# Reordering the PE and ACT queues of a fused two-layer transformer block: z transpose, output projection, context product, weight rounds and second scores

## The reference

```python
x = x + wkv(w, u, layernorm(x), ctx)              # a recurrence over the rows
x = x + fake_quant_ffn(layernorm(x))              # 256x256, 8-bit fake quantisation
x = x + cross_and_self_attention(layernorm(x), ctx)
x = x + gated_linear_attention(layernorm(x))
```

```python
ln = _ln(x)                                        # "z"; then 4 scaled copies rounded to fp8
q, k, v, qx = four projections of the fp8 copies   # 16 heads of 128; 8 groups of k and v
kx, vx = split(cond @ w_kv_x)                      # from the context
q, k, qx, kx = each normalised over its head's 128 features
core = softmax(q k^T / sqrt(128)) v
xout = softmax(qx kx^T / sqrt(128)) vx
x += fp8(concat(core, xout) / smooth) @ wproj^T * scales
```

## Time and profile before

| | us |
|---|---|
| median of 3 executions | 684.87 |
| lowest, highest | 682.72, 685.02 |
| profiled execution: its own time | 684.33 |
| profiled execution: span from first to last instruction | 682.5 |

### The profile page before, as it was taken

How to read it: one execution, slowest core, us unless ns; L and a number is a source line. 1 busy time by engine, 2 the same in 40 slices (tenths; PEclk the granted TensorE clock), 3 DMA queues, 4 the chain that set the end, 5 groups by cost and what they waited for, 6 DMA issues and landing times.

```text
span 682.5 us, 13253 instructions
## 1 busy us (share of the span) xinstructions
PE 614.7 (90%) x4523; PEld 492.6 (72%) x4567; DVE 528.4 (77%) x1305; ACT 401.6 (59%) x1339; POOL 250.1 (37%) x338
## 2 busy tenths in 40 slices
PE   4456999999999999989999999989999999999936
PEld 3245777777877878877788778768887788877725
DVE  7998688988786768858877788868664676868697
ACT  4255766767777646647667366567563666554531
POOL 2115664334333453323345433333332444430233
PEclk9997999999999999989999999999999999999977
DMA  8236452343672203331233222332342323110001
GB/s 269 79 148 215 149 167 71 104 163 119 210 259 101 101 15 105 109 104 74 105 122 103 90 101 101 101 102 101 102 162 100 102 101 101 16 33 1 1 0 62
DMA packets 36972, 72.86 MB, mean 107 GB/s; under 512 B 3342, under 2 KB 28586, under 8 KB 32810
## 3 DMA queue, kind: packets, MB, share of 16 engines
q1 hardware_dynamic: 36720, 72.00, 31.7%
q10 hardware_dynamic: 186, 0.02, 0.0%
HBM read 59.41 MB, written 12.60 MB: 106 GB/s over the span
## 4 chain that ended last, share of the span: by engine, by line
PE 73%; DVE 13%; issue 6%; ACT 5%; POOL 2%; DMA 0%; another core or an unknown queue 0%; DVEq 0%; POOLq 0%; ACTq 0%
PE bank L691 14%; PE bank L591 14%; PE bank L711 13%; PE bank L598 8%; PE bank L663 4%; PE bank L677 3%; PE bank L735 3%; PE bank L692 2%; PE bank L725 2%; PE bank L821 2%; PE bank L481 1%; PE bank L830 1%; DVE Cb L1749 1%; PE bank L750 1%; ACT KTt L1093 1%
## 5 line engine op out<-in xcount | busy, mean ns | idle before, releaser
L711 PEld LDWEIGHTS bank<-V,Pt 128*128 128x128 f32 x1024 | 127.7, 191 | 27.1 <-DVE Cb L1749 15.7
L1069 ACT ACTIVATE square<-bank 128x128 bf16<-128x128 f32 x372 | 98.4, 276 | 75.8 <-PE bank L591 46.7
L711 PE MATMUL bank<-V,Pt 128*128 128x129 f32 x1024 | 136.6, 276 | 2.2 <-DVE Cb L1749 1.2
L691 PE MATMUL bank<-QT,KTt 128*128 128x512 f32 x256 | 132.5, 599 | 2.9 <-POOL diag L1332 1.5
L1332 POOL TENSOR_TENSOR diag<-identb,nm 128x512 bf16<-128x512 bf16 x64 | 66.9, 1045 | 169.5 <-DVE nm L1734 169.4
L1052 ACT ACTIVATE Pt<-bank 128x512 f32<-128x512 f32 x128 | 76.8, 600 | 72.2 <-remote 46.3
L1734 DVE TENSOR_REDUCE nm<-bank 128x2 f32<-128x512 f32 x128 | 82.0, 682 | 36.2 <-PE bank L677 36.1
L1317 POOL TENSOR_TENSOR rs<-ve,mhalf 128x6 f32<-128x6 f32 x64 | 86.8, 1356 | 5.3
L591 PE MATMUL bank<-WQ,xq 128*128 128x256 f32 x512 | 80.4, 300 | 1.9 <-DVE xq L1645 1.3
L1749 DVE SCALAR_TENSOR_TENSOR Cb<-bank,ro,ism 128x128 bf16<-128x128 f32 x256 | 78.1, 347 | 4.5
L591 PEld LDWEIGHTS bank<-WQ,xq 128*128 128x128 f32 x512 | 68.1, 192 | 13.6 <-issue 7.6
(11 more groups left out here) (233 smaller groups left out, 1017.9 us busy)
## 6 DMA issues: line engine op xcount, KB each, us to landing
WQ<-wq_split SPq DMA_DIRECT2D x24, 1024.0 KB, 7.7
WH<-wh_split SPq DMA_DIRECT2D x24, 384.0 KB, 8.9
wq_split<-WQ SPq DMA_DIRECT2D x8, 1024.0 KB, 4.6
ism<-smooth_inverse SPq DMA_DIRECT2D x32, 256.0 KB, 6.4
wst<-in_L_xattn_wproj SPq DMA_DIRECT2D x16, 256.0 KB, 4.0
wh_split<-WH SPq DMA_DIRECT2D x8, 384.0 KB, 3.4
wst<-in_L_xattn_wq SPq DMA_DIRECT2D x8, 256.0 KB, 5.0
wst<-in_L_xattn_wqx SPq DMA_DIRECT2D x8, 256.0 KB, 5.1
```

The source lines that it names most:

```text
L691: nc.tensor.matmul(o[:], KTt[u % 2][:, x, t * P:(t + 1) * P], QT[u % 2][:, x, :], start=True, stop=False)
L711: last = nc.tensor.matmul(o[:, h * (P + 2):h * (P + 2) + P + 1], Pt[:, x, k, h * S + t * P:h * S + (t + 1) * P], V[u % 2][:, x, k, 0:P + 1 ...
L1069: last = A(square[:, t, h], head(t, h), ACT.Square, accum_out=ss[:, t, h:h + 1])
```

## The change

The instructions are the same; their order on PE and on ACT is another. DVE, POOL and SP keep theirs.

- `SCORES_FIRST` goes from 6 to 1: from unit 1 on, `scores(u, 0, 1)` follows `scores(u, 0, 0)` directly, ahead of `project(u + 1, 1)`, and so do the exponentials on ACT.
- The context product of tile 0 of unit `u + 2` (`project_values`) leaves the end of `project(u + 2, 0)` and stands ahead of `guard(u + 1, 0)`.
- In the units with `g == 1` from batch 1 on, `weigh(u, 0, 0)` goes ahead of `project_out(b - 1, 1)`, and `turn_outputs(u - 1)` behind `turn(u + 1)`; ACT's copy of it stands between the third and the fourth part of `evacuate`.
- `turn_z` stands behind `project(u + 2, 0)` in batches 1 and 2, and so does its read on ACT.
- In unit 7 the three weight rounds each come one place earlier, the first right behind `project(8, 0)`. In unit 6 ACT reads the second round ahead of `over_scales`.

```diff
@@ -233,7 +233,7 @@
 
         NARROW_BEHIND = {0: 3, 1: 4, 4: 6, 5: 7}
 
-        SCORES_FIRST = 6
+        SCORES_FIRST = 1
 
         def round_of(u, i):
 
@@ -608,7 +608,16 @@
                 else:
                     pe.wait_ge(s[f"ring{u % RING}_loaded"], loads_before(u))
 
-            def project(u, t):
+            def project_values(u):
+
+                b, g = divmod(u, G)
+                if u < G:
+                    pe.wait_ge(s["wc_evac"], u + 1)
+                if g == 0:
+                    pe.wait_ge(s["v_evac"], b + 1)
+                project_context(u, 0)
+
+            def project(u, t, context=True):
 
                 b, g = divmod(u, G)
                 if t == 0:
@@ -628,8 +637,10 @@
                 for p in range(2, 4):
                     if g == 0 and t == 0:
                         pe.wait_ge(s["xq4_ready"], 4 * b + p + 1)
-                    project_head(u, t, p)
-                project_context(u, t).then_inc(s["qkv_done"], 1)
+                    last = project_head(u, t, p)
+                if context:
+                    last = project_context(u, t)
+                last.then_inc(s["qkv_done"], 1)
 
             def project_first_context():
 
@@ -884,6 +895,8 @@
                     scores(u, 0, 1)
                 if u + 1 == G:
                     project(u + 1, 0)
+                    for r in round_of(u, 0):
+                        weights(*r)
                 project(u + 1, 1)
                 if 1 in steps:
                     turn_context(nb)
@@ -894,33 +907,38 @@
                 if u < SCORES_FIRST:
                     scores(u, 0, 1)
                 scores(u, 1, 0)
+                weigh(u, 0, 0)
                 if g == 1 and b:
                     project_out(b - 1, 1)
-                weigh(u, 0, 0)
-                if u >= 1 and not (g == 1 and b):
+                elif u >= 1:
                     turn_outputs(u - 1)
                 scores(u, 1, 1)
                 if 5 in steps:
                     ffn(nb)
                 weigh(u, 0, 1)
+                for r in round_of(u, 1 if u + 1 == G else 0):
+                    weights(*r)
+                turn(u + 1)
                 if g == 1 and b:
                     turn_outputs(u - 1)
-                for r in round_of(u, 0):
+                weigh(u, 1, 0)
+                for r in round_of(u, 2 if u + 1 == G else 1):
                     weights(*r)
-                turn(u + 1)
-                weigh(u, 1, 0)
-                for r in round_of(u, 1):
-                    weights(*r)
+                if u + 2 != G and u + 2 < UNITS:
+                    project_values(u + 2)
                 guard(u + 1, 0)
                 weigh(u, 1, 1)
-                if 6 in steps:
+                if 6 in steps and not b:
                     turn_z(nb)
                 if u + 2 != G and u + 2 < UNITS:
-                    project(u + 2, 0)
+                    project(u + 2, 0, False)
                 if 0 in steps:
                     turn_h(nb)
-                for r in round_of(u, 2):
-                    weights(*r)
+                if 6 in steps and b:
+                    turn_z(nb)
+                if u + 1 != G:
+                    for r in round_of(u, 2):
+                        weights(*r)
                 guard(u + 1, 1)
                 if g == 0 and u:
                     project_out(b - 1, 0)
@@ -1184,28 +1204,34 @@
                 if u >= 1 and not (u % G == 1 and u > G):
                     outputs(u - 1)
                 exps(u, 1, 1)
-                for r in round_of(u, 0):
+                for r in round_of(u, 1 if u + 1 == G else 0):
                     weights(*r)
+                if 1 in steps:
+                    differences(nb, 0, 1)
+                evacuate(u + 1, range(3))
                 if u % G == 1 and u > G:
                     outputs(u - 1)
-                if 1 in steps:
-                    differences(nb, 0, 1)
-                evacuate(u + 1)
-                if 7 in steps:
+                evacuate(u + 1, (3,))
+                if 7 in steps and u >= G:
                     over_scales(nb, (2, 3))
-                for r in round_of(u, 1):
+                for r in round_of(u, 2 if u + 1 == G else 1):
                     weights(*r)
+                if 7 in steps and u < G:
+                    over_scales(nb, (2, 3))
                 if 1 in steps:
                     differences(nb, 2, 3)
-                if 6 in steps:
+                if 6 in steps and u < G:
                     turned_z(nb)
                 if u + 2 != G and u + 2 < UNITS:
                     squares(u + 2, 0)
                     values(u + 2, 0)
                 if 0 in steps:
                     turned_h(nb)
-                for r in round_of(u, 2):
-                    weights(*r)
+                if 6 in steps and u >= G:
+                    turned_z(nb)
+                if u + 1 != G:
+                    for r in round_of(u, 2):
+                        weights(*r)
 
             u = UNITS - 1
             exps(u, 0, 0)
```

## The result

The changed kernel takes **672.3 us** by the median of 4 executions (672.11 to 672.55). The kernel before, measured beside it, takes 684.62 (682.72 to 685.02). The ratio is 0.9826, 95% interval 0.9807 to 0.9845: 12.3 us faster. The prediction was 669.5, range 665.5 to 676.5. So sign and range hold, and 2.8 us of the forecast gain are missing. The profiled execution took 672.11, its span is 670.3 us.

A forecast was written before the change was run, and what follows sets the result against it. PE was taken to bound the kernel, except in batch 0 and some units of batches 1 and 2, where DVE's chain is as long. Terms summed to 15.0 us off 684.33, 669.3; forecast 669.5, range 665.5 to 676.5.

The forecast's parts named there:

- z transposes: Units 12 and 20: projection and context product fill PE's wait ahead of the transposes of z, 2 x 2.64 = 5.3 us.
- Clock: Unit 12: with the long wait gone, the stretch at the lower clock behind it goes too, 2.8 us, from 0 to 2.8.
- Context product at the guards: Ends of units 0, 8, 9, 16, 17, 25: it fills PE's waits at the guard, 0.9 plus five times 0.4, 2.9 us.
- What that move delays: First guard up to 0.92 us later; DVE's gapless chains in units 10, 14, 18, 22 lose: -0.4 us, between -3 and +1.
- Batch 0: Units 1 to 5: losses from later guards and gains from earlier second scores cancel, 0 us, between -2.5 and +1.5.
- Unit 9 and its like: Units 9, 17, 25: output transposes no longer wait for their bank, 3 x 0.72 = 2.2 us, between 1.6 and 2.4.
- Weight rounds: Units 6 and 7: PE's waits for ACT ahead of weight rounds go, 2.2 us net, between 0.8 and 3.0.
- DVE takes the place of the waits: Rival: DVE's gapless chains in batches 0 to 2 leave 8.5 us of the gain, 676; chance 0.20 for 671.5 to 677.
- Slower: Rival: the first guard's 0.92 us passes whole through DVE and POOL in 29 places, about 695 us; chance 0.04.
- The clock is not won: Rival: the clock drop is chance or comes again at unit 1's longer diagonal wait, 672.3 us; chance 0.12.

The follow-up runs named there:

- z_only: The kernel before with only the z transposes, and ACT's read of them, moved behind the projection in batches 1 and 2: 675.78 us against 683.27, ratio 0.9885.
- after_pool_late: The changed kernel with POOL's first difference of the recurrence also waiting for DVE's pair of maxima with shifted rows: 670.51 us, ratio 0.98.

## Why the prediction was right in sign and 2.8 us off

Point by point, forecast against the lengths of bodies:

- **z transposes, 5.3.** Bodies 12 and 20 give 2.55 each without the clock, 5.1. Right; and DVE's scaling was not put off by the moved guard.
- **Clock, 2.8.** Right in the profile (2.80), and close for the median: z_only wins 7.5 by the medians of the chip, 5.5 of it without the clock, which leaves 2.0 (2.4 by the ratio). That the profile of before held a whole drop is luck: four profiles with both waits lost 2.80 + 0, 1.58 + 0, 0 + 1.65 and 1.50 + 1.61 us in bodies 12 and 20, so the picture of one drop in one place was wrong. In the rule of the Trainium skill that was weighed (TensorE: Matmul & The Clock Gate, What's actually happening) the half rate is the default and activity releases it; that each of two equal waits must then cost a drop was the prediction's own reading of it. That a drop can come at both is shown (1.50 and 1.61); that one must is refuted by the zeros, each behind a full wait.
- **Context product at the guards, 2.9.** The guards' records are 0.62 in the five later places, as forecast, and still 0.86 in body 0, where 0.9 was to be won and 0.69 was. The others gave 0.49 in bodies 8 and 16 (seen only once the loss there is gone), and 0.30 in bodies 9, 17 and 25: 2.6 in all. Nearly right.
- **What that move delays, 0.4 lost.** This is the step that failed. Bodies 14 and 22 are longer by 0.3 as worked out, 10 and 18 by 0.38 instead of 0.2, and body 29, which was not looked at, by 0.27. Bodies 13 and 21 win some 0.2 instead of 0.3, and nine others 0.06 each. What is missing altogether is 0.95 us in each of bodies 8 and 16, 1.9 us: 0.84 of each is DVE held up by POOL. The prediction followed DVE's queue with fixed durations, and one of them went from 0.48 to 1.32. The trace of before had such a case: the first step of the fp8 rounding (L1761), 0.42 us by the median, took 1.36 at the ends of bodies 8 and 16, beside a POOL instruction.

```profile
232.70 1.09 POOL L1297 TENSOR_TENSOR tmp<-tmp,vT 128x512 f32<-128x512 f32 x1
232.70 1.36 DVE L1761 TENSOR_SCALAR Cb<-Cb 128x1024 bf16<-128x1024 bf16 x1
```

  With it the term comes to -2.6 instead of -0.4, two thirds of the 3.3 us that the bodies fall short of the forecast (15.0 less 11.7).
- **Batch 0, 0.** The second scores gave 0.6 to 0.95, and the later guards took 1.4 (body 0 aside), so -0.8 by the first figure. The loss of 0.7 foreseen at the second weighing of unit 3 is there: it starts 9.46 us after the body's start instead of 8.70. What wasn't seen is the next step in the same body. PE and DVE of the changed kernel:

```profile
129.24 0.94 PE L722 MATMUL bank<-V,Pt 128*128 128x129 f32 x6 [0.20 <-DVE Cb L1775]
...
137.42 0.49 PE L562 MATMUL bank<-cen,wst 128*128 128x128 f32 x2 [0.38 <-DVE rest L1733]
...
134.32 1.29 DVE L1760 TENSOR_REDUCE nm<-bank 128x2 f32<-128x512 f32 x2 [0.63 <-PE bank L688]
...
136.25 1.11 DVE L1733 SCALAR_TENSOR_TENSOR rest<-bank,vec,WH 128x128 f32<-128x128 f32 x4
```

  DVE waits 0.63 for the later guard (L688) before its maxima; behind them in its queue are an output scaling and the read of a weight round (L1733), and the next round on PE (L562) needs that bank: 0.38. 0.76 and 0.38 make up body 3's 1.12. I listed what is queued on DVE behind the maxima, but not the weight round. Of body 5's 0.38 the trace shows the place: its output transposes (L736) wait 0.49 for the last step of DVE's rounding (L1791). In body 6, 0.34 longer, the second weighing waits 0.16 for an output scaling; the rest is open.
- **Unit 9 and its like, 2.2.** 1.03 in each of three bodies less 0.29 in two: 2.5, just above the upper bound of 2.4. The gap from the weighing to the next step was 1.68 less 0.89 = 0.79, the upper end; 0.24 more came from the steps around. The give-back in body 10 was not named.
- **Weight rounds, 2.2.** 1.13 and 1.09: 2.2. Right.
- **The rivals.** "DVE takes the place of the waits" describes the missing part, at a third of its size. "Slower" needed 0.55 us a place in 29 places; six places lose over 0.35 and nine gain 0.06. Its mechanism is real in body 3. "The clock is not won" has 672.3, the very time measured, and still isn't the reason: its price was a drop that comes again, and no stretch of the units ran below 1.00 in the changed kernel's profile.
- **The sum itself.** 684.33 less 15.0, plus the 0.5 that the prediction names, is 669.8, not 669.5.

By bodies these are 5.1 + 2.8 + 2.6 - 2.6 - 0.8 + 2.5 + 2.2 = 11.8, against 11.7 in the table; the other 0.5 of the 12.2 us between the two profiled executions, 684.33 and 672.11, lie outside the units. Most of it is the stretch from body 31 on, 68.2 us before and 67.8 now; it varies from 67.8 to 68.5 between profiles of kernels that don't differ there, so it isn't the change. Without the clock and that stretch the queues' new order is worth 8.9 us.

## What to carry to other kernels

Fill a gap with a step only in the units that have the gap: the same line moved in all units lost 2.0 us, and moved in four of them won 2.0. (Of the 2.0 lost, 1.8 were the meeting with POOL; where that was kept away the move in all units came out even, 670.51 against 670.26.) Where an engine has no gap, follow everything that is queued behind a delayed instruction, up to the next thing that another engine waits for, and not only the chain that bound before. And when a shift of some tenths of a microsecond costs more than itself, look in the trace for an instruction whose duration changed.

## What the runs showed of the hardware

- **A POOL instruction can hold up one of DVE.** The same DVE instruction (128x256, float32, two operands from SBUF) took 0.48 us, and 1.32 when a POOL tensor operation of 1.04 us began together with it; keeping them apart gave the 0.84 us back. So the engines do not meet at semaphores alone, as the description of the core above has it. The Trainium skill (SBUF — State Buffer, SBUF: two separate sides) says that a VectorE operation with two SBUF inputs and a GpSimd operation that reads SBUF share a port pair, which the first holds for its whole instruction while the other is fully blocked. The trace agrees in the main: the surplus of 0.84 is 0.2 less than the 1.04 us for which POOL's instruction ran. What the traces show is an end: the held instruction ends 0.28 us after POOL's. So it is in bodies 8 and 16, in the row of L1761 above (234.06 less 233.79 is 0.27, by times rounded to 0.01), which reads one operand and not two (a case that the sentence above leaves out), and in all 134 DVE instructions of the units, over the 13 profiles read, that took over 1.2 times, and over 0.1 us more than, the median of their kind. In after_pool_late the meeting is only moved, to the next DVE pair of this kind (L1578), which takes 1.62 us at 221.84 instead of 0.88, and costs PE nothing there.

```profile
221.84 1.62 DVE L1578 SCALAR_TENSOR_TENSOR tmp<-tmp,vec 128x256 f32<-128x256 f32 x2
```

- **A drop of the clock need not be whole.** Behind equal waits of 2.97 us the bodies lost 0, 1.28, 1.50, 1.58, 1.61, 1.65 or 2.80 us, by execution, and behind waits of 2.1 us 0 or 1.54. Behind none of the waits in the changed kernel's units, of which the longest is 1.11, was there a drop. The drops explain most of the spread of the kernel before, 2.3 to 3.9 us against 0.3 to 1.1 without these waits.
